# Sixteen attention heads' scores, minima and exps made inside the first layer's expert tiles

## The chip, the cores and the metric

One core of a Trainium2 chip runs the whole program in one launch. The metric is the device time of that core in microseconds, the median of several executions. TensorE does the matmuls and the transposes, VectorE (DVE in the profile) and ScalarE (ACT) the work on rows, GpSimd (POOL) the gathers by index, SyncE (SP) issues most DMAs. PSUM has eight banks of 128 partitions by 512 fp32 numbers, and TensorE writes nowhere else.

## What is computed

The network has two layers over 1024 tokens (4 sequences of 256) of width 256. Each layer multiplies an attention block by a gate from a mixture of experts; both read the same normalised rows.

```python
xn = _layernorm(x)
s = _L0_attn_ref(xn, Wq, Wk, Wv, Wo)          # softmax attention, 16 heads of 16, rope, causal
g = _silu(_L0_ffn_ref(xn, ...))               # 16 experts, the best 4 for each token
x = x + s * g
# second layer: linear attention and 32 experts, built in the same way

# inside _L0_ffn_ref, for each expert
gate = jnp.minimum(gate, LIMIT); up = jnp.clip(up, -LIMIT, LIMIT)
glu = gate * jax.nn.sigmoid(gate * ALPHA)
out = jnp.einsum('etd,edh->eth', (up + 1.0) * glu, down_proj) + down_proj_bias
out = (out * router_scores.T[:, :, None]).sum(axis=0)
# inside _L0_attn_ref
attn = jax.nn.softmax(where(causal, q @ k.T / 4, -inf)); out = attn @ v
```

With 4 sequences and 16 heads there are 64 heads to attend, each with a 256 by 256 causal matrix.

## The kernel before

Tokens are sorted by expert into rows of `NT0` = 47 tiles of 128. For each tile POOL gathers the rows, TensorE turns them (`turn`, bank 0 or 1), ACT copies them to SBUF (`turn`, L708), TensorE makes gate and up in 16 matmuls (`up`, L1169, bank 2 or 3), DVE adds biases and clips in four instructions and multiplies in a fifth (`gate`, L1642 to L1647), ACT makes the sigmoid (`gate`, L720), DVE multiplies by it (L1653), TensorE makes the down product in 4 matmuls (`down`, L1185, bank 6 or 7), and ACT weighs and stores it (`weigh`, L756). SP fetches each tile's expert weights four tiles ahead.

`run_tiles` writes out one order of work for each engine. For step u it goes through a list of (lag, every, work) and calls the work of tile u minus lag. TensorE's step u is: up of tile u-1, turn of tile u, down of tile u-3. ACT's step u is: turn of u, weigh of u-4, sigmoid of u-1, place heads, bias rows. DVE's is the gate of tile u-1. Engines work in their own order and meet only at semaphores, so whatever stands behind a waiting instruction waits too. POOL rotates queries and keys (rope) between the gathers of tiles 7 to 28; SP and ACT then place heads by DMA into `heads_qk`, the first half by tile 27.

When the tiles end, the attention starts, again in an order by steps, `run_pairs`: step u handles pairs of heads. `scores(n)` makes four heads' scores in 16 matmuls (L1264, banks 0 to 3), two for each head, packed by 32 rows of the array; for n of 1 or more it first waits until the minima of all four heads before are read out of the banks (`s_mx`, 8n). `smallest` on DVE masks and copies a head to SBUF and finds its minima (L1769, two instructions and their accumulator reads for each head), ACT makes the exps in place (`probs`, L835, two for each head), TensorE turns a head in three transposes (`turn_probs`, L1289, banks 4 and 5), DVE copies one head of the pair and ACT the other (L1778, L845), TensorE attends (`attend`, L1307, bank 6), and so on to the projection (L1334). Scores, minima and exps of pair p come in step p (the second exp in p+1), turning the pair in step p+2. Only `scores(0)` stands in the tile stretch, between the downs of its last two tiles. The ring of probabilities `pr` holds six heads.

Meanwhile POOL gathers the weighted rows back, 32 gathers (L595) that start when the last tile is stored; step 33 of DVE needs the last of them (`row_sums`). ACT holds the functions of one table at a time: `ahead` is a one-column activation that loads the next table early.

```python
def run_steps(total, body, stages):
    for u in range(min(lag for lag, _, _ in stages), total + max(lag for lag, _, _ in stages)):
        for lag, every, work in stages:
            v = u - lag
            if v % every == 0 and 0 <= v < total:
                work(v // every, v // every % (body // every))
```

## Time and profile before

| | us |
|---|---|
| median of 3 runs | 426.87 |
| lowest and highest | 425.85, 428.62 |
| span of the profiled execution | 462.5 |
| TensorE busy in it | 421.1 (91%) |
| VectorE busy in it | 329.8 (71%) |
| ScalarE busy in it | 234.4 (51%) |
| GpSimd busy in it | 216.2 (47%) |
| mean granted TensorE clock | 0.963 of 2.4 GHz |

The profiled execution is 35.6 us longer than the median of the plain runs. Times of instructions are read in it, and so a difference worked out from them is one in the profiled execution. An engine is busy while an instruction is in it; a matmul's end is modelled, and neighbours overlap, so start to start says more of TensorE than the duration. The granted clock is 1.00 at 2.4 GHz and 0.50 at 1.2 GHz.

### The profile page before, as it was taken

What the parts mean: (1) busy time and instruction counts of PE and PEld (TensorE: products, weight loads), DVE (VectorE), ACT (ScalarE), POOL (GpSimd) and SP (SyncE); (2) the same over time, 40 slices, a digit from 0 to 9 for tenths busy, and PEclk for the clock granted to TensorE, in tenths of its full rate; (3) what the DMA queues carried; (4) which work ended last, traced back from release to release, by engine and by line L of the source; (5) the groups of instructions that cost most, each with busy time, mean ns of one, the idle gap of its engine ahead of it and who ended that gap; (6) DMA issues with size and microseconds to landing.
All of it is one profiled execution on the core that took longest, in us unless ns stands there. A gap on an engine that the chain in (4) does not pass through costs nothing.

```text
span 462.5 us, 10086 instructions
## 1 busy us (share of the span) xinstructions
PE 421.1 (91%) x3213; PEld 327.6 (71%) x3213; DVE 329.8 (71%) x1135; ACT 234.4 (51%) x596; POOL 216.2 (47%) x208
## 2 busy tenths in 40 slices
PE   8899999899999998998989899958988999969696
PEld 4757899798999997656666684646766774645585
DVE  5886699978866667588999988525576664344685
ACT  3373233434433436878899636315566568124421
POOL 2023688767643320778880101655576602747400
PEclk9999999999999999589999999979999999979889
DMA  8937888888999982379776760233555523323202
GB/s 246 409 142 240 319 275 268 250 258 279 282 312 308 316 277 69 79 195 211 150 172 187 268 210 7 85 87 114 166 145 149 165 92 116 107 63 104 68 23 68
DMA packets 42274, 84.17 MB, mean 182 GB/s; under 512 B 7136, under 2 KB 27104, under 8 KB 41584
## 3 DMA queue, kind: packets, MB, share of 16 engines
q1 hardware_dynamic: 30656, 60.99, 39.6%
q0 software_dynamic: 9936, 20.85, 18.5%
q10 hardware_dynamic: 1632, 1.71, 1.1%
q8 instruction: 27, 0.44, 0.4%
q14 instruction: 23, 0.19, 0.1%
HBM read 65.81 MB, written 15.60 MB: 176 GB/s over the span
## 4 chain that ended last, share of the span: by engine, by line
PE 63%; DVE 14%; issue 8%; ACT 6%; another core or an unknown queue 4%; DMA 3%; SPq 1%; POOL 1%; ACTq 0%; DVEq 0%
PE ps L1169 14%; PE ps L1120 7%; PE ps L1185 7%; PE ps L1147 4%; PE ps L1289 4%; PE ps L964 3%; PE ps L1264 3%; PE ps L1106 3%; PE ps L1377 3%; ACT til L835 2%; PE ps L948 2%; PE ps L967 2%; DMA experts<-in_gu 2%; PE ps L1158 2%
## 5 line engine op out<-in xcount | busy, mean ns | idle before, releaser
L544 POOL DMA_INDIRECT til<-xn_rows,gidx x71 | 71.0, 999 | 98.1 <-PE ps L1158 43.4
L1169 PEld LDWEIGHTS ps<-til,experts 128*128 128x128 f32 x752 | 90.6, 192 | 8.1 <-issue 3.9
L1169 PE MATMUL ps<-til,experts 128*128 128x128 f32 x752 | 92.1, 276 | 3.2 <-DVE til L1645 1.5
L708 ACT ACTIVATE til<-ps 128x256 f32<-128x256 f32 x47 | 18.0, 382 | 66.2 <-PE ps L1158 66.2
L835 ACT ACTIVATE til<-til,mxs 128x128 f32<-128x128 f32 (+1 forms) x128 | 49.0, 453 | 0.0
L1185 PE MATMUL ps<-experts,til 128*128 x188 | 48.4, 381 | 0.0
L1120 PE MATMUL ps<-experts,til 128*64 x192 | 36.1, 345 | 9.4 <-issue 9.4
L756 ACT ACTIVATE til<-ps,wtile 128x256 f32<-128x256 f32 x95 | 42.0, 471 | 2.5 <-PE ps L1149 2.4
L1769 DVE CUSTOM_DVE_ANT_0 til<-ps,cst 128x128 f32<-128x128 f32 (+1 forms) x128 | 37.8, 352 | 5.7 <-PE ps L1264 3.3
L1120 PEld LDWEIGHTS ps<-experts,til 128*64 128x64 f32 x192 | 26.7, 144 | 15.5 <-issue 12.2
L1122 PE MATMUL ps<-xn,til 128*64 128x192 f32 x192 | 36.2, 345 | 0.0
L1289 PE MATMUL ps<-cst,til 128*128 128x128 f32 x192 | 31.3, 302 | 4.9 <-DVE til L1778 2.6
L1185 PEld LDWEIGHTS ps<-experts,til 128*128 128x128 f32 x188 | 32.1, 190 | 2.8 <-issue 0.3
L1289 PEld LDWEIGHTS ps<-cst,til 128*128 128x128 f32 x192 | 22.7, 152 | 15.5 <-issue 10.4
L544 POOL DMA_INDIRECT wqkv<-xn_rows,gidx x24 | 26.0, 1084 | 16.1 <-PE ps L1106 5.8
L1642 DVE TENSOR_SCALAR til<-ps,bcol 128x128 f32<-128x128 f32 x47 | 16.4, 348 | 23.9 <-PE ps L1169 23.0
L595 POOL DMA_INDIRECT rou<-sorted_rows,slotu x16 | 20.4, 1276 | 24.9 <-DMA sorted_rows<-til 19.4
L582 POOL DMA_INDIRECT rou<-sorted_rows,slotu x16 | 16.1, 1005 | 29.2 <-DMA sorted_rows<-til 20.3
L1660 DVE TENSOR_TENSOR til<-til,ps 128x192 f32<-128x192 f32 x24 | 8.5, 354 | 29.2 <-ACT til L727 22.5
L1366 PE MATMUL ps<-att,experts 128*128 128x512 f32 x64 | 29.0, 602 | 0.0
L1647 DVE SCALAR_TENSOR_TENSOR til<-til 128x256 f32<-128x256 f32 x47 | 27.9, 593 | 1.6
L1653 DVE TENSOR_TENSOR til<-til 128x256 f32<-128x256 f32 x47 | 27.1, 576 | 2.6 <-issue 0.5
(240 smaller groups left out, 959.4 us busy)
## 6 DMA issues: line engine op xcount, KB each, us to landing
experts<-in_gu SPq DMA_DIRECT2D x47, 512.0 KB
sorted_rows<-til SPq DMA_DIRECT2D x95, 128.0 KB
experts<-in_gu SPq DMA_DIRECT2D x8, 768.0 KB
experts<-in_dn SPq DMA_DIRECT2D x4, 1024.0 KB, 11.0
experts<-in_dn SPq DMA_DIRECT2D x8, 384.0 KB
experts<-att SPq DMA_DIRECT2D x44, 32.0 KB
til<-xn_rows,gidx POOLq DMA_INDIRECT x71
xr<-in_x SPq DMA_DIRECT2D x2, 512.0 KB, 4.2
```

Of the source, the lines that this page charges most:

```text
L544: po.indirect_dma_start(to, None, xn_dram[s.n], bass.IndirectOffsetOnAxis(ap=gidx[:, t:t + 1], axis=0))\
L756: ac.activation(ybuf[:, j, :], y, ACT.Copy, scale=wtile[:, t:t + 1])\
L835: ins = ac.activation(pr[h % len(pr)][:, cols], pr[h % len(pr)][:, cols], ACT.Exp, bias=mxs[:, h % len(pr), tt:tt + 1], scale=-1.0)
L1120: pe.matmul(ps[0:HALF_ROWS, 2 + p % 2, at], xgT1[:, p % 2, c, k, 0:HALF_ROWS], gu[:, bass.ds(e * (KD * w) + k * w, w)], start=(k == 0), st ...
L1122: mm = pe.matmul(ps[HALF_ROWS:P, 2 + p % 2, at], xgT1[:, p % 2, c, k, HALF_ROWS:P], gu_second[t % 4][:, k * w:(k + 1) * w], start=(k == 0) ...
L1169: mm = pe.matmul(ps[:, b0, m * P:(m + 1) * P], gw[:, j, k * w + m * P:k * w + (m + 1) * P], xgT[:, j % 2, k, :], start=(k == 0), stop=(k = ...
L1185: mm = pe.matmul(ps[:, 6 + j % 2, 0:D], hT[0:s.FP, j % 2, k, :], dn[0:s.FP, bass.ds(e * (s.KF * D) + k * D, D)], start=(k == 0), stop=(k = ...
L1289: mm = pe.transpose(ps[:, 4 + h % 2, n * P:(n + 1) * P], pr[h % len(pr)][:, n * P:(n + 1) * P], ident)
L1366: mm = pe.matmul(ps[:, n % 2 + 2 * w, :], wsgu_sb[:, k, w * SH + m * P:w * SH + (m + 1) * P], L[1].xnT[:, k, h * 512:(h + 1) * 512], start ...
L1647: ve.scalar_tensor_tensor(out=ubuf[:, j % 2, :], in0=ubuf[:, j % 2, :], scalar=1.0 - LIMIT, in1=gbuf[:, j % 2, :], op0=ALU.max, op1=ALU.mu ...
L1653: ve.tensor_tensor(hT[:, j % 2, :, :], ubuf[:, j % 2, :].rearrange("p (m t) -> p m t", m=2), sig[:, j % 2, :].rearrange("p (m t) -> p m t" ...
L1769: ve.tensor_tensor_reduce(out=pr[h % len(pr)][:, cols], in0=ps[:, h % 4, cols], in1=maskz[:, (1 - tt) * P:2 * P], scale=1.0, scalar=3.0e38 ...
```

## The change

Sixteen of the 64 heads (`AHEAD`, the first sequence) get their scores, minima and exps in the expert tiles' steps. TensorE's step gets `heads_ahead` at its end, `scores(0)` to `scores(3)` behind tiles 31, 35, 39 and 43; DVE's step gets `smallest_of_head` at its end, one head in each of tiles 32 to 45 and two in tile 46; ACT's gets `probs_ahead` at its end, one tile later. Banks for these scores are 1, 4, 5 and 7. For that, turns use bank 0 only and down products bank 6 only, so both wait for the copy of the tile just before, and ACT's `weigh` moves from second to first place in its step. The sigmoid becomes a Tanh of half the argument, its 1 is added in the last multiply (a SCALAR_TENSOR_TENSOR for the TENSOR_TENSOR), and the 0.5 goes into the tiles' weights; the two table loads around (Sigmoid, then Exp) go. Sixteen buffers for probabilities are laid in free memory, one of them new. In the attention the ring holds 14, and scores, minima and exps of the other 48 heads come four steps earlier against the turning than they did.

```diff
+        pr_ring = [til[:, 384 * n:384 * (n + 1)] for n in range(6)] + pr_ahead[8:16]
+        AHEAD = 16
+        AHEAD_TILE = 31
+        AHEAD_BANKS = (1, 4, 5, 7)
+        def heads_at(t):
+            h = t - AHEAD_TILE - 1
+            return () if h < 0 else (h, h + 1) if t == NT0 - 1 else (h,)
@@ ScalarE
-                ac.activation(ahead[:, :], ones_e[:, 0:1], (ACT.Sigmoid, ACT.Silu)[s.n])
+                if s.n == 1:
+                    ac.activation(ahead[:, :], ones_e[:, 0:1], ACT.Silu)
-                    ac.activation(sig[:, j % 2, 0:s.F], gbuf[:, j % 2, :], ACT.Sigmoid, scale=ALPHA)\
+                    ac.activation(sig[:, j % 2, 0:s.F], gbuf[:, j % 2, :], ACT.Tanh, scale=ALPHA / 2)\
-                    if s.n == 0 and t == NT0 - 3:
-                        ac.activation(ahead[:, :], ones_e[:, 0:1], ACT.Exp)
-                    run_tiles(s, [(0, 1, turn), (0, 1, last_wide), (4, 1, weigh), (1, 1, gate), (1, 1, place_heads), (2, 1, bias_rows)])
+                    run_tiles(s, [(4, 1, weigh), (0, 1, turn), (0, 1, last_wide), (1, 1, gate), (1, 1, place_heads), (2, 1, bias_rows), (2, 1, probs_ahead)])
+            def probs_of_head(h):
+                ac.wait_ge(s_mx, h * 2 + 2)
+                for tt, cols in ((0, slice(0, P)), (1, slice(P, 3 * P))):
+                    ins = ac.activation(probs_of(h)[:, cols], probs_of(h)[:, cols], ACT.Exp,
+                                        bias=mxs[:, h % 6, tt:tt + 1], scale=-1.0)
+                ins.then_inc(s_exp, 1)
-            run_pairs([(13, 8, ...), (1, 1, probs(1)), (2, 1, probs_turned_act),
-                       (8, 4, turned0), (0, 1, probs(0)), (4, 2, attended),
+            run_pairs([(13, 8, ...), (-3, 1, probs(1)), (2, 1, probs_turned_act),
+                       (8, 4, turned0), (-4, 1, probs(0)), (4, 2, attended),
@@ TensorE
-                    if t >= 2:
-                        pe.wait_ge(s.xgT_ready, t - 1)
+                    if t >= 1:
+                        pe.wait_ge(s.xgT_ready, t)
-                        mm = pe.transpose(ps[:, j % 2, k * P:(k + 1) * P], xg[:, j, k * P:(k + 1) * P], ident)
+                        mm = pe.transpose(ps[:, 0, k * P:(k + 1) * P], xg[:, j, k * P:(k + 1) * P], ident)
-                    if t >= 2:
-                        pe.wait_ge(s.y_ready, t - 1)
+                    if t >= 1:
+                        pe.wait_ge(s.y_ready, t)
-                        mm = pe.matmul(ps[:, 6 + j % 2, 0:D], hT[0:s.FP, j % 2, k, :],
+                        mm = pe.matmul(ps[:, 6, 0:D], hT[0:s.FP, j % 2, k, :],
-                    run_tiles(s, [(1, 1, up), ..., (3, 1, first_heads), (3, 1, down)])
+                    def heads_ahead(t, j):
+                        if t >= AHEAD_TILE and (t - AHEAD_TILE) % 4 == 0:
+                            scores((t - AHEAD_TILE) // 4, 0)
+                    run_tiles(s, [(1, 1, up), ..., (3, 1, down), (1, 1, heads_ahead)])
-                        mm = pe.matmul(ps[:, r, cols], ...)
+                        mm = pe.matmul(ps[:, AHEAD_BANKS[r] if n < AHEAD // 4 else r, cols], ...)
-            run_pairs([(0, 2, lambda n, j: scores(n, j) if n >= 1 else None), (2, 1, turn_probs), ...
+            run_pairs([(-4, 2, lambda n, j: scores(n, j) if n >= AHEAD // 4 else None), (2, 1, turn_probs), ...
@@ VectorE
-                    ve.tensor_tensor(hT[...], ubuf[...], sig[...], ALU.mult).then_inc(s.h_ready, 1)
+                    ve.scalar_tensor_tensor(out=hT[...], in0=sig[...], scalar=1.0,
+                                            in1=ubuf[...], op0=ALU.add, op1=ALU.mult).then_inc(s.h_ready, 1)
-                    run_tiles(s, [(1, 1, bias_columns), (1, 1, gate), (0, 1, weights(s)), (0, 1, bias_weights)])
+                    run_tiles(s, [(1, 1, bias_columns), (1, 1, gate), (0, 1, weights(s)), (0, 1, bias_weights), (1, 1, heads_ahead)])
-            run_pairs([(0, 1, smallest), (2, 1, probs_turned), ...
+            run_pairs([(-4, 1, smallest), (2, 1, probs_turned), ...
```

## Rows read from the trace of the kernel before

**Rows 1.** Windows by stage: start:end length, busy (instructions) PE PEld DVE ACT POOL, PEclk, DMA.
```profile
92.20:177.60 85.40, 84.80 (x646) 80.69 (x647) 63.15 (x174) 34.74 (x97) 38.51 (x42) 1.00 0.86 278
177.60:185.50 7.90, 6.49 (x62) 4.90 (x60) 5.39 (x25) 6.30 (x18) 0.00 (x0) 1.00 0.26 86
185.50:201.50 16.00, 15.42 (x125) 10.24 (x121) 10.63 (x56) 12.25 (x35) 12.04 (x9) 0.57 0.61 137
201.50:247.80 46.30, 41.34 (x491) 28.27 (x487) 42.05 (x202) 41.13 (x118) 34.05 (x25) 1.00 0.79 181
247.80:259.40 11.60, 10.22 (x115) 7.27 (x111) 11.30 (x51) 10.26 (x29) 1.05 (x1) 1.00 0.67 227
```

**Rows 2.** Timeline of one expert tile: start, length, engine, line, operation, idle before it.
```profile
166.14 1.95 PE L1169 MATMUL ps<-til,experts 128*128 128x128 f32 x16
...
168.12 0.35 DVE L1642 TENSOR_SCALAR til<-ps,bcol 128x128 f32<-128x128 f32 x1 [0.82 <-PE ps L1169]
168.14 1.03 PE L1185 MATMUL ps<-experts,til 128*128 x4
168.34 0.38 ACT L708 ACTIVATE til<-ps 128x256 f32<-128x256 f32 x1 [1.81 <-PE ps L1158]
...
168.62 0.47 ACT L756 ACTIVATE til<-ps,wtile 128x256 f32<-128x256 f32 x1
...
169.01 1.95 PE L1169 MATMUL ps<-til,experts 128*128 128x128 f32 x16
...
169.74 0.42 DVE L1653 TENSOR_TENSOR til<-til 128x256 f32<-128x256 f32 x1
```

**Rows 3.** Timeline from the last tile's gate and up to the first turned heads.
```profile
177.61 1.95 PE L1169 MATMUL ps<-til,experts 128*128 128x128 f32 x16
...
181.34 1.28 ACT L761 ACT_TABLE_LOAD   x1
...
183.84 0.28 DVE L1769 CUSTOM_DVE_ANT_0 til<-ps,cst 128x128 f32<-128x128 f32 x1
...
184.07 2.86 ACT L835 ACTIVATE til<-til,mxs 128x128 f32<-128x128 f32 x8
184.40 0.08 DVE L1769 DVE_READ_ACCUMULATOR2_ANT mxs<- 128x1 f32 x1
...
184.63 0.94 PE L1264 MATMUL ps<-experts 16*128 16x128 f32 x16 [1.41 <-DVE mxs L1769]
...
185.50 1.29 PE L1289 MATMUL ps<-cst,til 128*128 128x128 f32 x6
```

**Rows 4.** Page, costliest groups: the two multiplies of the expert gate, all 47 tiles.
```profile
L1647 DVE SCALAR_TENSOR_TENSOR til<-til 128x256 f32<-128x256 f32 x47 | 27.9, 593 | 1.6
L1653 DVE TENSOR_TENSOR til<-til 128x256 f32<-128x256 f32 x47 | 27.1, 576 | 2.6 <-issue 0.5
```

**Rows 5.** Timeline, TensorE: turned heads at steps 8, 28 and 33 of the attention.
```profile
201.47 0.87 PE L1289 MATMUL ps<-cst,til 128*128 128x128 f32 x6
...
247.80 0.87 PE L1289 MATMUL ps<-cst,til 128*128 128x128 f32 x6
...
259.38 0.88 PE L1289 MATMUL ps<-cst,til 128*128 128x128 f32 x6
```

**Rows 6.** Timeline, GpSimd (last gather back) and ScalarE (a Tanh among the exps).
```profile
241.27 1.53 POOL L595 DMA_INDIRECT experts<-sorted_rows,slotu  x1 [0.30 <-issue]
...
213.32 0.63 ACT L859 ACTIVATE rou<-rou 128x512 f32<-128x512 f32 x1
```

**Rows 7.** Windows of 2 us around a fall and a rise of the clock, later in the kernel.
```profile
304.00:306.00 2.00, 0.60 (x4) 0.33 (x3) 0.00 (x0) 0.00 (x0) 0.47 (x1) 0.82 0.40 117
...
312.00:314.00 2.00, 2.00 (x20) 1.21 (x16) 1.20 (x5) 1.03 (x3) 0.00 (x0) 0.98 0.20 55
```

**Rows 8.** TensorE: a gap in the second layer's tiles, and 2 us around it.
```profile
323.26 0.37 PE L1120 MATMUL ps<-experts,til 128*64 x1 [1.37 <-issue]
...
322.00:324.00 2.00, 0.74 (x10) 0.69 (x12) 2.00 (x7) 2.00 (x6) 1.65 (x2) 1.00 0.52 145
```

More of the change, by code:

```diff
@@ L170, in build_program @@
         dn_second = [wo0_sb[0:F1, n, :] for n in range(2)] + [xn_free[0:F1, 1536 + n * D:1536 + (n + 1) * D] for n in range(2)]
-        pr = [til[:, 384 * n:384 * (n + 1)] for n in range(6)]
+        pr_more = sb("pr_more", [P, 384])
         prT = [til[:, 384 * n:384 * (n + 1)] for n in range(6, 9)] + [big[:, 14336 + 384 * n:14336 + 384 * (n + 1)] for n in range(5)]
@@ L241, in build_program @@
         shift1 = (rou[:, 2048:3072].rearrange("p (t n) -> p t n", t=4), stk.rearrange("p a w t -> p (a w) t"))
+        xnT0_free = att[:, 6144:8192]
+        pr_ahead = ([rou[:, 2048 + 384 * n:2048 + 384 * (n + 1)] for n in range(4)]
+                    + [stk[:, 1, :, :].rearrange("p w t -> p (w t)")[:, 0:384], pr_more[:, :]]
+                    + [xn_free[:, 384 * n:384 * (n + 1)] for n in range(5)] + [xnT0_free[:, 384 * n:384 * (n + 1)] for n in range(5)])
+        pr_ring = [til[:, 384 * n:384 * (n + 1)] for n in range(6)] + pr_ahead[8:16]
         mxs = sb("mxs", [P, 6, 2])
@@ L398, in build_program, with probs_of @@
         EARLY_ROWS = ((0, 4), (4, 6), (6, 8))
+        AHEAD = 16
+        AHEAD_TILE = 31
+        AHEAD_BANKS = (1, 4, 5, 7)
+        def probs_of(h):
+            return pr_ahead[h] if h < AHEAD else pr_ring[(h - AHEAD) % len(pr_ring)]
+        def heads_at(t):
+            h = t - AHEAD_TILE - 1
+            return () if h < 0 else (h, h + 1) if t == NT0 - 1 else (h,)
+        assert [h for t in range(NT0) for h in heads_at(t)] == list(range(AHEAD))
         ONCE = BATCH * HEADS // 2
@@ L832, in work @@
                     h = 2 * p + half
-                    ac.wait_ge(s_mx, h * 2 + 2)
-                    for tt, cols in ((0, slice(0, P)), (1, slice(P, 3 * P))):
-                        ins = ac.activation(pr[h % len(pr)][:, cols], pr[h % len(pr)][:, cols], ACT.Exp,
-                                            bias=mxs[:, h % len(pr), tt:tt + 1], scale=-1.0)
-                    ins.then_inc(s_exp, 1)
+                    if h >= AHEAD:
+                        probs_of_head(h)
                 return work
@@ L1221, in tiles @@
                 if s.n == 0:
-                    def first_heads(t, j):
-                        if t == NT0 - 1:
-                            scores(0, 0)
-                    run_tiles(s, [(1, 1, up), (0, 1, turn), (0, 4, experts), (0, 1, begin), (1, 1, weights), (1, 1, bias_rows), (3, 1, first_heads), (3, 1, down)])
+                    def heads_ahead(t, j):
+                        if t >= AHEAD_TILE and (t - AHEAD_TILE) % 4 == 0:
+                            scores((t - AHEAD_TILE) // 4, 0)
+                    run_tiles(s, [(1, 1, up), (0, 1, turn), (0, 4, experts), (0, 1, begin), (1, 1, weights), (1, 1, bias_rows), (3, 1, down), (1, 1, heads_ahead)])
                 else:
@@ L1283, in turn_probs @@
             def turn_probs(p, j):
+                if p == 0:
+                    pe.wait_ge(s_mx, 2 * AHEAD)
                 for h in (2 * p, 2 * p + 1):
@@ L1710, in tiles, with heads_ahead @@
                 if s.n == 0:
-                    run_tiles(s, [(1, 1, bias_columns), (1, 1, gate), (0, 1, weights(s)), (0, 1, bias_weights)])
+                    def heads_ahead(t, j):
+                        if t == AHEAD_TILE + 3:
+                            ve.wait_ge(s_rope, NTT)
+                        for h in heads_at(t):
+                            smallest_of_head(h)
+                    run_tiles(s, [(1, 1, bias_columns), (1, 1, gate), (0, 1, weights(s)), (0, 1, bias_weights), (1, 1, heads_ahead)])
                 else:
@@ L1748, in tiles, with smallest_of_head @@
                     run_double_tiles([(0, first_copies), (1, turned_four), (0, gate_four), (0, copy_four), (1, biases), (3, products)])
+            def smallest_of_head(h):
+                ve.wait_ge(s_sc, h + 1)
+                if h >= 6:
+                    ve.wait_ge(s_exp, h - 5)
+                if h >= AHEAD + 6:
+                    ve.wait_ge(s_pT, h - len(pr_ring) + 1)
+                bank = AHEAD_BANKS[h % 4] if h < AHEAD else h % 4
+                for tt, cols in ((0, slice(0, P)), (1, slice(P, 3 * P))):
+                    ve.tensor_tensor_reduce(out=probs_of(h)[:, cols], in0=ps[:, bank, cols], in1=maskz[:, (1 - tt) * P:2 * P],
+                                            scale=1.0, scalar=3.0e38, op0=ALU.add, op1=ALU.min,
+                                            accum_out=mxs[:, h % 6, tt:tt + 1]).then_inc(s_mx, 1)
             link(ve.memset(ones_e[:, :], 1.0))
@@ L1764, in smallest @@
                 for h in (2 * p, 2 * p + 1):
[L1765 to L1771 removed]
+                    if h >= AHEAD:
+                        smallest_of_head(h)
             def probs_turned(p, j):
```

32 lines of the change are left out of this document (15 added, 17 removed).

## The prediction

> **What bounds the kernel now.** I read the windows by stage first, because a mean over the span mixes stretches with different limits. From 92 us to the last expert tile TensorE is busy 84.80 of 85.40 us and DVE 63.15 [rows 1]: this stretch goes at TensorE's pace, and everything added to TensorE's order there is paid in full. The attention is another thing. From 201.5 to 247.8 us DVE is busy 42.05 of 46.3, TensorE 41.34 and ACT 41.13 [rows 1]: three engines at about 90%, none of them free. The 16 us before that ran at a granted clock of 0.57. If the clock has only the levels 1.00 and 0.50, that is 13.8 us at 1.2 GHz (0.86 of 16.0), with TensorE busy 15.42 us [rows 1]. So the change takes work from a stretch where all three are loaded and gives it to one where DVE and ACT have room and TensorE has none.
>
> The timeline of one tile comes second. Call T the start of an up. The next up starts at T+2.87, DVE starts the gate at T+1.98, and its last multiply ends at T+4.02 (169.74 + 0.42 against 166.14) [rows 2]. DVE thus needs 2.04 us of 2.87. The timeline of the hand-over comes third: from the last up (177.61) to the first turned head (185.50) go 7.9 us, with a TensorE gap of 1.41 us that DVE's minima end [rows 3].
>
> **The edits that cost nothing.** One bank for turns: the up of tile t already waits for the same copy (L708), and TensorE's next turn stands behind that up, so the new wait is always fulfilled. One bank for downs: down of tile t now waits for weigh of t-1. ACT turns at T+2.20, makes the tanh, then in the last tiles two exps (0.72 a head: 2.86 for eight [rows 3]), then weighs (0.47 [rows 2]). All four are 0.38 + 0.42 + 0.72 + 0.47, about 2.0 us, taking a tanh like DVE's multiply of as many columns; they end near T+4.2, or T+1.3 of the next tile, and down comes there at T+2.0, right behind the up and the turn (168.14 [rows 2]). It has 0.7 us to spare, and if that went, it would add to each tile. The other multiply: a SCALAR_TENSOR_TENSOR of the same columns costs 27.9 us for 47 against 27.1 [rows 4], at most 0.8 in all; I take 0. Tanh for Sigmoid: a Tanh stands among exps with no table load before it [rows 6], so Tanh and Exp can alternate. The removed load at 181.34 is 1.28 us of ACT [rows 3]; its gain is in the hand-over below. The other removed load lies before the tiles, where TensorE sets the pace: 0 (bounds 0 and -1.3).
>
> **The scores in the tiles.** Four `scores`, 0.87 us each (184.63 to 185.50 [rows 3]), are 3.5 us on the engine that bounds. DVE's added head takes 0.64 us (183.84 to 184.48 [rows 3]), 2.68 with the gate, under 2.87: DVE keeps up.
>
> Then the wait. `scores(n)` needs the minima of head 4n-1. That head's minima stand in DVE's step for tile 31+4n, behind the gate of this tile, and this gate needs the up of the same tile. `scores(n)` stands in TensorE's step of the same tile. So TensorE, done with turn and down at T+2.87, stands until DVE has ended the gate (T+4.02), the head (0.64) and the signal has passed (184.48 to 184.63, 0.15 [rows 3]): T+4.81. That is 1.94 us of waiting, for n = 1, 2 and 3, and the next up is behind it in TensorE's order, then everything that waits for it. `scores(0)` has no such wait. Sum of the stretch: 4 x 0.87 + 3 x 1.94 = 9.3 us. Bounds: without waits 3.5, with 2.3 us each 10.4; I take 9.3, since its parts are read next to each other.
>
> **The hand-over.** From the last up: gate ends at 4.02, DVE's two heads (14 and 15) at 5.3, ACT's exps of head 15 at 6.0, then weigh of tile 45 (0.47), down of tile 46 (0.87), which needs it in the one bank: 7.4, first turned head at 7.5 against 7.9 before. -0.4. TensorE has one up and three downs in this time, so it stands idle for more than 2.5 us. I expect the clock to fall here as it did before.
>
> **The attention**, from first turn to the turn of step 33. Before: 185.50 to 259.38, 73.9 us [rows 3, 5]. Steps 2 to 8 took 16.0. Steps 2 and 3 now hold no scores, minima or exps; I take 1.5 off for the two (a scores at each level of the clock would be 0.87 and 1.7) and leave the rest at the low clock: 14.5 (bounds 12.4 with a high clock, at 2.3 a step, and 16.0). Steps 8 to 28 took 46.3. They hold the same work as before, because what moved is the head start: 24 pairs still need their minima and exps by step 27. The exps are no longer fresh when the turn comes, so a little waiting goes: 45.5 (bounds: DVE's own 42.1, and 46.3). Steps 28 to 33 took 11.6 [rows 5] and lose a scores and the last exps. TensorE's own work there is 10.22 busy less 0.87, 9.3 [rows 1]; I take 9.6 (bounds 9.3, 11.6). Sum 69.6, which is -4.3. TensorE's work over all of it is 8.8 (15.42 at 0.57) + 41.3 + 10.2 - 1.7 = 58.6 us at full clock and 65.5 with 13.8 us of it at half: 69.6 is 94% of that, so there is not much more to get while the clock is low. The gathers don't bind: the last is issued at 242.8, 57.3 us after the first turn [rows 6, 3], and step 33 comes at 69.6.
>
> **Sum.** +9.3 - 0.4 - 4.3 = +4.6 us on the profiled span of 462.5. The plain runs are 35.6 us shorter and I can't see where; I carry the difference over unchanged: 426.9 + 4.6 = 431.5 us, 1.1% slower.
>
> **Rivals.**
>
> The clock falls in the tiles. A gap of 1.37 us left the clock at 1.00 in the second layer [rows 8]; a gap of 1.41 us followed by scores was followed by the fall at the hand-over [rows 1, 3]. The waits here are 1.94 us and followed by scores too, which speaks for it; for the rest of the four tiles TensorE is dense, which speaks against it. A low spell in the second layer ran from 305.3 to 312.1 by the means 0.82 and 0.98, 6.8 us [rows 7], and costs 3.4 us where TensorE bounds. Three falls: +10.2, 441.7 us; one: 434.9.
> The Trainium skill, "TensorE: Matmul & The Clock Gate", section "A second HAM failure mode: psum-queue depth-cycling", says that a kernel that cycles through PSUM banks and lets TensorE idle briefly between groups of matmuls can swing between both clock levels. That is the pattern which this change makes in the tiles; by that rule the sum is the rival's 441.7, and the row of the 1.37 us gap does not agree with it.
>
> The attention comes free of its bound, and the kernel is faster. The mechanism: with 16 heads' probabilities ready, the first turns come in an unbroken row, TensorE keeps or soon regains 2.4 GHz, and DVE sets the pace. DVE's busy time in the attention is 10.63 + 42.05 + 11.30 = 64.0 us [rows 1], less 12 heads by 0.64, 56.3. (Four heads lay before the first turn already.) At the 91% of the long window this is 61.9 us, at the 97% of the last one 58.0; TensorE's 58.6 stands beside it. Net 9.3 - 0.4 - 12.0 = -3.1, 423.8 us, and at best 7.0 less, 419.9. The point from which it decides: an attention below 65.0 us makes up for the tiles. Against it: two downs spaced by waits stand right before the turns, and TensorE was busy 15.42 of 16 us before and still had the low clock.
>
> The waits are not there. If something hides them, 3.5 - 0.4 - 4.3 = -1.2, 425.7 us, no change. Only a gate that DVE could finish before TensorE's down would do that, and 4.02 against 2.87 speaks plainly against it.
>
> **How the numbers follow.** Forecast 52%, with its own range of 427.5 to 436 (waits of 1.5 to 2.3 us, attention of 66 to 73); clock falling in the tiles 15%; attention unbound 23%; waits absent 10%. A measurement of this kernel can tell about 1% from no change, 4.3 us. Slower by over 1%: 28 of the forecast's 52 (its middle lies just over the line), the 15 and 3 of the rest, 46%. Within 1%: 24, 10 of the unbound attention, 5, 39%. Faster: 13 and 2, 15%. The range reaches from 421.5, where nearly all of the unbound attention is in, to 440, with two falls of the clock in.
>
> **What would show it.** In the timeline of the changed kernel: TensorE idle for about 1.9 us before three of the four early `scores`, ended by DVE's accumulator read; tile starts 5.7 us apart there and 2.87 elsewhere. The window from 92 us to the last tile's up 9.3 us longer, at clock 1.00. From the last up to the first turned head about 7.5 us; a clock near 0.5 behind it. From the first turn to step 33's about 70 us. It is wrong in the tiles if the waits are short or the clock is below 1.00 there, in the attention if it takes under 66 us, and in the carrying over if the profiled spans differ by 4 to 5 us and the medians do not.

## The result, and the profile after

| | before | after |
|---|---|---|
| median, us | 427.55 | 447.67 |
| lowest and highest | 425.85, 428.62 | 446.14, 449.91 |
| ratio after / before, 95% interval | | 1.0446 (1.0405 to 1.0486) |
| span of the profiled execution | 462.5, and 425.9 in a second one | 446.9 |

The changed kernel is slower by 20.1 us, where 4.6 had been forecast. On another chip the same two kernels gave 449.13 against 427.9 (below).

The kernel before was profiled again (`before_again`): 427.73 us, span 425.9. Its first profile, on which the prediction rests, was an unusually slow execution, so the comparison is made with the second. The windows by stage of it, the counterpart of [rows 1] and the stages behind (start:end, length, busy time of TensorE, its weight loads, VectorE, ScalarE and GpSimd with instructions, granted clock, share of the DMA engines, GB/s):

```profile
92.20:133.10 40.90, 40.90 (x316) 39.38 (x316) 33.70 (x84) 17.56 (x48) 26.42 (x29) 1.00 0.90 288
133.10:176.20 43.10, 43.10 (x332) 41.51 (x332) 29.72 (x92) 17.09 (x51) 12.04 (x14) 1.00 0.84 277
176.20:184.00 7.80, 6.39 (x61) 4.85 (x59) 5.33 (x25) 6.20 (x18) 0.00 (x0) 1.00 0.27 87
184.00:200.00 16.00, 14.84 (x153) 10.15 (x150) 12.92 (x72) 14.40 (x42) 11.95 (x9) 0.79 0.63 139
200.00:251.90 51.90, 47.91 (x570) 33.73 (x568) 50.28 (x240) 49.03 (x139) 34.88 (x26) 1.00 0.86 211
251.90:270.50 18.60, 17.84 (x130) 15.26 (x127) 16.29 (x70) 7.23 (x20) 1.88 (x2) 1.00 0.62 202
```

The same view of the changed kernel, cut at the same events of the work:

```profile
92.20:138.40 46.20, 43.32 (x326) 40.73 (x325) 35.67 (x90) 21.27 (x50) 28.09 (x30) 1.00 0.86 273
138.40:192.40 54.00, 49.18 (x396) 44.83 (x395) 36.87 (x144) 27.60 (x74) 11.94 (x14) 0.97 0.69 213
192.40:200.90 8.50, 5.81 (x30) 4.44 (x29) 4.71 (x21) 5.44 (x16) 0.00 (x0) 0.84 0.14 46
200.90:216.90 16.00, 15.63 (x151) 10.55 (x149) 10.97 (x56) 11.29 (x32) 9.89 (x8) 0.77 0.58 135
216.90:267.00 50.10, 45.77 (x535) 32.70 (x534) 45.66 (x206) 43.74 (x122) 36.92 (x27) 1.00 0.87 209
267.00:291.20 24.20, 20.86 (x131) 17.66 (x127) 16.23 (x70) 7.34 (x20) 1.40 (x2) 0.86 0.56 185
```

The cuts are the up of tile 31, the last up, the first turned head, the turn of step 33, and layer two's first wide product. Between them stand the 21.0 us by which the two profiled spans differ:

| stage | before, us | after, us | difference | predicted |
|---|---|---|---|---|
| start to up of tile 31 | 133.1 | 138.4 | +5.3 | 0 |
| up of tile 31 to last up | 43.0 | 54.0 | +10.9 | +9.3 |
| last up to first turned head | 7.9 | 8.5 | +0.6 | -0.4 |
| attention, to the turn of step 33 | 67.9 | 66.2 | -1.7 | -4.3 |
| to layer two's first wide product | 18.6 | 24.2 | +5.6 | 0 |
| the rest of layer two | 155.4 | 155.7 | +0.3 | 0 |

TensorE fills both of the first windows of before (40.90 of 40.90, 43.10 of 43.10). After, it stands idle for 2.9 and 4.8 us there. In the second it has the scores to make besides; the first holds slightly more of the tiles' work, since both views begin at 92.20 and the changed kernel is 3.2 us late by then (tile 17's up at 95.18 against 92.02). TensorE's waits from 38 to 200 us, changed kernel (waiting line, releaser, us in total, times, longest):

```profile
PE ps L1211 <- ACT til L776: 6.8, 6, 1.5
PE ps L1292 <- DVE mxs L1796: 4.8, 3, 1.6
PE ps L1195 <- DMA experts<-in_gu: 1.3, 1, 1.3
```

L1292 is the scores in the tiles and L1211 the down product, which was L1185 in [rows 2]. In the second profile of before, TensorE waits 1.5 us for VectorE and 0.3 us for expert weights in these tiles, and for nothing else.

**The second tile of scores.** TensorE's timeline there, the counterpart of [rows 2] (start, length, engine, line, operation, idle before it):

```profile
152.96 1.03 PE L1211 MATMUL ps<-experts,til 128*128 x4
155.60 0.94 PE L1292 MATMUL ps<-experts 16*128 16x128 f32 x16 [1.60 <-DVE mxs L1796]
156.46 3.13 PE L1195 MATMUL ps<-til,experts 128*128 128x128 f32 x16
159.38 0.63 PE L1184 MATMUL ps<-cst,til 128*128 128x128 f32 x2
159.81 1.44 PE L1211 MATMUL ps<-experts,til 128*128 x4
161.08 1.95 PE L1195 MATMUL ps<-til,experts 128*128 128x128 f32 x16
...
155.46 0.08 DVE L1796 DVE_READ_ACCUMULATOR2_ANT mxs<- 128x1 f32 x1
```

and a window of 2 us in the next tile:

```profile
158.00:160.00 2.00, 2.00 (x11) 2.00 (x11) 0.37 (x2) 0.00 (x0) 0.00 (x0) 0.50 0.05 18
```

The wait is where the prediction put it, and VectorE's accumulator read ends it. Behind it one up takes 3.13 us instead of 1.95: TensorE's clock fell to its lower level (0.50 in the window), and this tile lasts 4.62 us, where the tiles behind the other scores take 2.97: 1.65 us lost. The waits of 1.61 us before the scores at 171.46 and at 185.68 were followed by ups of the usual length.

**The end of the attention.** The chain of waits (start, us, what):

```profile
260.01 1.53 POOL experts L614
261.54 0.30 issue
261.85 10.62 DMA experts<-sorted_rows,slotu
272.59 0.69 DVE rou L1838
273.48 0.43 DVE stk L1830
273.96 0.69 PE ps L1356 x2
```

and the two lines of the timeline that belong to it:

```profile
272.59 0.69 DVE L1838 TENSOR_TENSOR rou<-rou,experts 128x512 f32<-128x512 f32 x1 [3.26 <-DMA experts<-sorted_rows,slotu]
...
273.96 0.69 PE L1356 MATMUL ps<-cst,stk 128*128 128x128 f32 x2 [2.59 <-DVE stk L1830]
```

The last gather was issued at 261.85, 61.0 us after the first turned head, and its rows were used 10.6 us later. VectorE waited 3.26 us for them in `row_sums` of the last sequence, the normalisation of the same sums stands behind it, and TensorE waited 2.59. In this last window TensorE's clock is 0.86 with 20.86 us busy, against 1.00 and 17.84 before: 3.0 us of the stage's 5.6 are the clock that fell behind the wait, 2.6 the wait. In `before_again` the last gather is issued at 242.60 and the same sum starts at 254.20, 11.6 us later, with no wait.

### The profile page after: what moved, and what is told of

The parts are those of the page before. It is cut to its first block, busy times and chain, and to the rows that moved or that the text cites. A ratio compares the mean times of both kernels' runs of the same rounds, so it can differ in the third digit from the quotient of the medians.

```text
span 446.9 us, 10085 instructions
## 1 busy us (share of the span) xinstructions
PE 416.4 (93%) x3213; PEld 325.8 (73%) x3213; DVE 332.1 (74%) x1135; ACT 239.6 (54%) x592; POOL 213.6 (48%) x208
## 3 DMA queue, kind: packets, MB, share of 16 engines
q0 software_dynamic: 9936, 20.85, 18.1%
## 4 chain that ended last, share of the span: by engine, by line
PE 61%; DVE 12%; DMA 12%; POOL 6%; issue 4%; ACT 2%; SPq 1%; ACTq 1%; POOLq 0%; DVEq 0%
PE ps L1195 14%; DMA experts<-sorted_rows,slotu 8%; PE ps L1146 6%; PE ps L1211 6%; PE ps L1396 6%; PE ps L1173 4%; PE ps L990 3%; PE ps L1407 3%; PE ps L1132 3%; POOL experts L614 3%; PE ps L974 2%; POOL rou L614 2%; DVE til L1677 2%; DMA experts<-in_gu 2%; PE ps L993 2%
## 5 line engine op out<-in xcount | busy, mean ns | idle before, releaser
L1211 PE MATMUL ps<-experts,til 128*128 x188 | 50.8, 394 | 7.0 <-ACT til L776 6.8
L1211 PEld LDWEIGHTS ps<-experts,til 128*128 128x128 f32 x188 | 32.9, 195 | 12.3 <-issue 9.5
L1148 PE MATMUL ps<-xn,til 128*64 128x192 f32 x192 | 33.8, 329 | 0.0
L1146 PE MATMUL ps<-experts,til 128*64 x192 | 33.7, 329 | 0.0
L740 ACT ACTIVATE til<-til 128x256 f32<-128x256 f32 x47 | 19.6, 417 | 20.7 <-DVE til L1673 19.3
L1677 DVE SCALAR_TENSOR_TENSOR til<-til 128x256 f32<-128x256 f32 x47 | 29.2, 622 | 1.6
L1683 DVE SCALAR_TENSOR_TENSOR til<-til 128x256 f32<-128x256 f32 x47 | 27.0, 575 | 3.6 <-PE ps L1211 2.2
L614 POOL DMA_INDIRECT experts<-sorted_rows,slotu x16 | 25.2, 1576 | 9.0 <-DMA experts<-sorted_rows,slotu 5.0
L563 POOL DMA_INDIRECT wqkv<-xn_rows,gidx x24 | 24.4, 1018 | 10.2 <-issue 5.8
L601 POOL DMA_INDIRECT rou<-sorted_rows,slotu x16 | 15.4, 965 | 24.0 <-DMA sorted_rows<-til 19.4
L1148 PEld LDWEIGHTS ps<-xn,til 128*64 128x64 f32 x192 | 25.3, 137 | 0.0
L1173 PE MATMUL ps<-experts,til 96*64 x96 | 22.7, 379 | 0.5 <-ACT til L776 0.5
L1292 PE MATMUL ps<-experts 16*128 16x128 f32 (+1 forms) x256 | 15.7, 362 | 5.8 <-DVE mxs L1796 5.8
## 6 DMA issues: line engine op xcount, KB each, us to landing
experts<-in_dn SPq DMA_DIRECT2D x4, 1024.0 KB, 11.7
```

Of the source, the lines that this page charges most:

```text
L563: po.indirect_dma_start(to, None, xn_dram[s.n], bass.IndirectOffsetOnAxis(ap=gidx[:, t:t + 1], axis=0))\
L614: po.indirect_dma_start(rows[:, i, :], None, ys_dram[s.n], bass.IndirectOffsetOnAxis(ap=slotu[s.n][:, i * TOPK + k:i * TOPK + k + 1], axis=0),
L740: ac.activation(sig[:, j % 2, 0:s.F], gbuf[:, j % 2, :], ACT.Tanh, scale=ALPHA / 2)\
L1146: pe.matmul(ps[0:HALF_ROWS, 2 + p % 2, at], xgT1[:, p % 2, c, k, 0:HALF_ROWS], gu[:, bass.ds(e * (KD * w) + k * w, w)], start=(k == 0), st ...
L1148: mm = pe.matmul(ps[HALF_ROWS:P, 2 + p % 2, at], xgT1[:, p % 2, c, k, HALF_ROWS:P], gu_second[t % 4][:, k * w:(k + 1) * w], start=(k == 0) ...
L1173: pe.matmul(ps[0:HALF_ROWS, 6 + p % 2, at], hT1[:, p % 2, c, 0:HALF_ROWS], dn[0:F1, bass.ds(e * D, D)], start=True, stop=True)
```

## The experiments

Twelve runs follow, two of them repeats. Differences in us are between medians; the kernel before had 427.6 to 429.3 on the chips they ran on, so the ratio to it is given too. The diffs are abridged: the reading side of a moved bank, changed semaphore counts and lines without weight for the argument are left out.

**The kernel before again.**

> The kernel before, unchanged, for a second profile of it. The first profiled execution had a span of 462.5 us where plain runs took 427. If that execution was an odd one, this profile has a span near 426 us and differs from the first mostly behind 300 us, in the second layer's tiles; then all comparisons behind 300 us go against this one. If profiling itself stretches this kernel, the span is again near 460 us.

Measured: 427.73 us, span 425.9. Its windows stand in the section above.

**The changed kernel again.**

> The changed kernel once more, unchanged, beside the kernel before on the same chip, as the reference for the runs with one edit undone. If its 447.7 us against 427.6 hold on another chip, the ratio is 1.0446 within 0.4%, about 448 us beside 429, and the three single edits (9.5, 4.7 and 5.4 us) sum to 19.6 where the three together gave 18.1. If the first time was high by the chip it ran on, the ratio is near 1.040 and the sum of the single edits falls to that of the three together.

Measured: 449.13 us, ratio 1.0489 (1.0454 to 1.0524), before 427.9. The loss is not one chip's, and if anything it is larger. In this profile tile 36 takes its usual 2.97 us behind the wait before `scores(1)`, and the low clock comes behind the wait before `scores(2)` instead (tile 40 lasts 4.62 us there, 2.97 in the first profile). The three variants below that keep the waits show one fall (`after_late_weights`, tile 36), one (`after_two_down_banks`, tile 44) and two (`after_fewer_gathers`, tiles 36 and 44): 6 falls behind 15 waits of 1.6 us in five profiles. Two more things differ from the first profile. TensorE waits 2.2 us for expert weights at tile 4 and tile 4 then lasts 4.59 us, and the attention takes 64.8 us with a clock of 0.95 in its first 16 us, where the first profile had 66.2 and 0.77.

**The waits taken away.** Scores one tile later (the lag goes from 1 to 2; expectations further down call it two), when the minima are already there:

```diff
-  run_tiles(s, [(1, 1, up), ..., (3, 1, down), (1, 1, heads_ahead)])
+  run_tiles(s, [(1, 1, up), ..., (3, 1, down), (2, 1, heads_ahead)])
```

> The changed kernel with its four early score groups one step later in TensorE's order, so that the minima they need are already made. Theory 1 (three causes add up: waits before the scores, one bank for the downs, the gathers back at the end of the attention): the three waits of 1.6 to 1.7 us and the clock's fall behind the first of them (1.8 us) go, 6.7 us of the tile stretch, and because the gathers set the end of the attention and start with the last tile, nearly all of it arrives: 441 us. Theory 2 (what was lost lies behind the tiles alone, in the attention and its clock): under 2 us less than the changed kernel's 447.7. Theory 3 (TensorE's added work counts, not its waits): same as the changed kernel.

Measured: 438.22 us, ratio 1.0194 (1.0147 to 1.0240), 9.5 us less than the changed kernel. The window of the last tiles of layer one, and that of the first 16 us of the attention:

```profile
138.00:188.00 50.00, 50.00 (x417) 45.91 (x416) 38.64 (x149) 28.82 (x77) 12.76 (x15) 1.00 0.78 248
...
195.60:211.60 16.00, 14.75 (x189) 10.14 (x187) 12.91 (x67) 13.77 (x40) 10.01 (x8) 1.00 0.64 170
```

TensorE has no gap in the tiles. The 4.8 us of waits and the 1.65 us of the slow tile go, and from the up of tile 31 to the last up it is 47.3 us instead of 54.0. Two things more are shorter in this profile: the hand-over is 7.6 us instead of 8.5, and the clock is 1.00 instead of 0.77 in the first turns, so that the attention takes 63.4 us instead of 66.2. How much of this is the edit's is less sure: the changed kernel's own clock in these 16 us differs between executions (0.77 and 0.95). The profiled execution is also the slowest of the four, 441.5 us; it waited 2.4 us for expert weights at tile 4.

**Two banks for the down products** of the first 28 tiles (bank 7 is given to the scores only from tile 31 on):

```diff
+  ONE_BANK = 28
+  def down_bank(t): return 6 + t % 2 if t < ONE_BANK else 6
-  if t >= 1: pe.wait_ge(s.y_ready, t)
+  if t >= 2: pe.wait_ge(s.y_ready, t - 1 if t < ONE_BANK else t)
-  mm = pe.matmul(ps[:, 6, 0:D], ...)
+  mm = pe.matmul(ps[:, down_bank(t), 0:D], ...)
```

> The changed kernel with two banks for the down products of tiles 0 to 27, one from tile 28 on. Theory 1: in the stretch where GpSimd rotates and VectorE is late (tiles 4 to 26), down waits for the weighing of the tile just before, which stands behind the late gate in ScalarE's order; two banks give back up to 3.2 us of the 3.8 lost by tile 31: 444.5 us. Rival: the loss in this stretch comes from the new multiply (a SCALAR_TENSOR_TENSOR beside GpSimd's rotations) or from ScalarE weighing first; then the tiles 0 to 31 are as late as in the changed kernel and the time stays within 1 us of 447.7.

Measured: 443.0 us, ratio 1.0333 (1.0270 to 1.0395), 4.7 us less. The up of tile 31 starts at 134.61 instead of 138.42; from there to the last up it is 53.96 us in both, as it should be, for both have one bank there. What one bank costs in the last tiles this run can't tell; in the changed kernel's list of waits no down waits between 138 and 192 us, and the next run, without the heads, has 43.0 us there as before. The attention is 1.7 us shorter in this profile (64.5 us, clock 0.94 in its first 16 us), but so it is in a variant that is the same as the changed kernel up to there (64.4 us, 0.94, in `after_fewer_gathers`). Of the 3.8 us at tile 31, 0.7 stood already at the first up (38.76 against 39.46). From the up of tile 5 to that of tile 31 the changed kernel takes 82.3 us, this one 78.8 and `before_again` 77.9: 3.5 us belong to the bank, and 0.9 us stay with two banks, their cause not tested.

**One bank on the kernel before**, for turns and for downs, with ScalarE's weighing first; heads and gate as before:

```diff
-  mm = pe.transpose(ps[:, j % 2, ...], ...)        # waits for xgT_ready, t - 1
+  mm = pe.transpose(ps[:, 0, ...], ...)            # waits for xgT_ready, t
-  mm = pe.matmul(ps[:, 6 + j % 2, 0:D], ...)       # waits for y_ready, t - 1
+  mm = pe.matmul(ps[:, 6, 0:D], ...)               # waits for y_ready, t
-  run_tiles(s, [(0, 1, turn), (0, 1, last_wide), (4, 1, weigh), ...])
+  run_tiles(s, [(4, 1, weigh), (0, 1, turn), (0, 1, last_wide), ...])
```

> The kernel before with one part of the change alone: in layer one one bank for the turns and one for the down products, and ScalarE's weighing of the products first among its steps. Heads and gate stay as before, the work is whole. Theory one (the single bank costs most of the 4.7 us that came back with two banks, in tiles 13 to 31 where VectorE's part of the gate runs late beside GpSimd's rotations): the last up product comes 3 to 5 us later and the time is 427.6 + 3 to 5 = 430.5 to 432.5. Theory two (the bank costs only together with the work that the heads add in the last tiles, or the hand-over): at most 1.5 us longer, 427.6 to 429.

Measured: 432.37 us, ratio 1.0085 (1.0040 to 1.0130), 3.1 us more than before on that chip. In the profile the tiles are 4.5 us longer by tile 31 than in `before_again` and not at all after it. From the up of tile 5 to that of tile 31 it takes 82.3 us, exactly what the changed kernel takes, so heads and gate have no part in this stretch. Five steps of 0.5 to 1.0 us, before the ups of tiles 14 to 26, make 3.9 of the 4.5. The hand-over is 1.0 us longer too (8.9 us) and the attention 1.9 shorter (66.0 us, at a clock of 1.00 against 0.79 in its first 16 us), which is why the median moves by less than the tiles. The timeline of the first, between the ups of tiles 13 (77.98) and 14 (82.60), on GpSimd, VectorE, TensorE and ScalarE:

```profile
76.86 1.34 POOL L571 TENSOR_TENSOR att<-att,experts 128x512 f32<-128x512 f32 x1
77.11 1.37 DVE L1653 TENSOR_TENSOR til<-til 128x256 f32<-128x256 f32 x1
...
77.98 1.95 PE L1169 MATMUL ps<-til,experts 128*128 128x128 f32 x16
...
78.41 0.88 DVE L1598 CAST experts<-rou 128x384 bf16<-128x384 f32 x1
...
79.32 0.70 DVE L1599 TENSOR_TENSOR rou<-rou,experts 128x128 f32<-128x128 f32 x1
...
80.32 0.34 DVE L1643 TENSOR_SCALAR til<-ps,bcol 128x128 f32<-128x128 f32 x1
...
80.70 0.42 ACT L720 ACTIVATE til<-til 128x256 f32<-128x256 f32 x1 [3.13 <-DVE til L1643]
...
81.02 0.46 ACT L756 ACTIVATE til<-ps,wtile 128x256 f32<-128x256 f32 x1
...
81.64 1.13 PE L1185 MATMUL ps<-experts,til 128*128 x4 [1.49 <-ACT til L756]
```

Read it upwards. TensorE's down waits for the weighing (L756). The weighing stands behind the sigmoid (L720) in ScalarE's order, the sigmoid waits 3.13 us for VectorE's bias and clip (L1643), and VectorE comes to tile 12's gate 5.1 us after the start of its up (80.05 against 74.97), where in a quiet tile it is 2.0 [rows 2]. It is late with a multiply that takes 1.37 us beside GpSimd's rotations, where it takes 0.42 in a quiet tile, and with a cast and a subtraction that split the routing weights. Before the change VectorE was late at this place too, but TensorE had one more bank to go on with, and waited less, for VectorE before its next up (`before_again`):

```profile
82.03 2.02 PE L1169 MATMUL ps<-til,experts 128*128 128x128 f32 x16 [0.83 <-DVE til L1645]
```

This run holds three edits at once, the two banks and ScalarE's order. That the down products' bank has most of the cost is told by the run before it; the other two were not tried alone. The Trainium skill, "GPSIMD Engine Reference", section "Specifications", says that VectorE and GpSimd share their interfaces to SBUF and that VectorE's instructions with two SBUF inputs contend; the 1.37 against 0.42 us agree.

**The last gathers taken away.** The last four of the 32 gathers are left out, so the last sequence's gate lacks part of its rows; on both kernels:

```diff
-  for r in range(2):
+  for r in range(2 if b < BATCH - 1 else 1):
```

> The changed kernel without the last four of the 32 gathers back (the second half of the experts' sum for the last sequence is left out, so its gate is wrong). Theory 1: at the end of the attention VectorE stands 3.3 us for the last gather's landing, TensorE and ScalarE behind it, and the clock falls for about 8 us; without four gathers of 1.8 us the sum is ready before it is asked for, 3.3 us of waiting and about 4 us of low clock go: 440 us. Rival (the end of the attention is bound by the engines, and the wait only takes the place of another): under 2 us less.

Measured: 441.66 us, ratio 1.0270 (1.0218 to 1.0321), 6.0 us less. No wait before the sum, and 18.6 us from step 33 to layer two instead of 24.2.

> The kernel before without the last four of the 32 gathers that bring the experts' rows back (the sums of the last sequence's second half then lack that part of the data; nothing else is left out). Theory one (before, the engines' work in the attention ends within about 1 us of the gathers, so the gathers bind only once the attention is shorter): the time is 0 to 1.5 us lower, 426 to 427.6, against 6.0 us that the same edit gave on the changed kernel. Theory two (the gathers bound the kernel before as much): 4 us lower or more, 423.5.

Measured: 428.02 us, ratio 0.9962 (0.9932 to 0.9993), 1.2 us less than before on that chip. The gathers bind the kernel before by 0.3 to 2.9 us, less than half of what they take from the changed one.

**The weights out of the gathers' way.** SP's order, on both kernels:

```diff
   sp.wait_ge(s_sc, BATCH * HEADS)
+  sp.wait_ge(s_sum, BATCH)
   for c in (5, 6, 7): gate_up_columns(c)
-  sp.wait_ge(s_sum, BATCH)
```

> The changed kernel with SP's wait for the last attention sums moved ahead of the loads of gate_up columns 5, 6 and 7, which are issued at 259.6 us in the changed kernel, while the last gathers are under way. The work is whole. Theory one (these loads share the DMA engines with the last gathers, which land 10.6 us after issue): the last gather lands sooner, the wait before row_sums(3) of 3.26 us goes to under 1 us, and the time falls by 2 to 4 us, if layer two's tiles do not then wait for columns 5 to 7. Theory two (the gathers are bound by their own transfers and by when they start): the wait stays within 0.7 us of 3.26, and the time is the same or longer by what the late columns cost.

Measured: 442.25 us, ratio 1.0290 (1.0229 to 1.0351), 5.4 us less; more than expected, because the clock stays up too. SP's issues (four of 768 KB: column 4, which no edit moves, and the three loads) and the 12 us up to step 33 in the changed kernel:

```profile
259.61 2.00 SPq L507 DMA_DIRECT2D experts<-in_gu  x4
...
255.00:267.00 12.00, 11.16 (x121) 8.27 (x120) 10.00 (x35) 8.12 (x22) 7.34 (x7) 1.00 1.00 279
```

The same with the loads held back, with the sum and the stage behind step 33:

```profile
258.39 12.04 SPq L507 DMA_DIRECT2D experts<-in_gu  x4
...
254.00:266.00 12.00, 11.16 (x122) 8.30 (x115) 10.00 (x34) 7.96 (x22) 7.30 (x6) 1.00 0.82 184
...
268.12 0.69 DVE L1838 TENSOR_TENSOR rou<-rou,experts 128x512 f32<-128x512 f32 x1
...
265.80:284.40 18.60, 17.84 (x130) 15.26 (x127) 16.30 (x70) 7.23 (x20) 1.88 (x2) 1.00 0.79 285
```

Column 4 goes out at 258.39 here too, the three loads from 268.91 on. The sum starts 7.3 us after the last gather's issue (260.79) instead of 10.6, with no wait at all, and the stage is 18.6 us, as before the change. Of the 12 us up to step 33 the DMA engines are busy for all in the changed kernel (share 1.00), and for 0.82 here. So the wait in the changed kernel was a collision: both the gathers' last rows and three loads of 768 KB want the DMA engines at one moment. Before the change they missed each other: in `before_again` the three loads are issued from 245.80 on, 3.2 us behind the last gather (242.60), in the changed kernel from 260.00 on, 1.9 us ahead of it (261.85). The Trainium skill, "DMA: Bandwidth & Descriptors", section "SWDGE vs HWDGE vs iDMA", says that each DMA engine goes round between the queues that GpSimd's and the other engines' transfers feed; a gather then slows when SP's queue is filled as well, and this pair of runs agrees.

> The kernel before with SP's wait for the last attention sums moved ahead of the loads of gate_up columns 5 to 7. The work is whole. Theory one (before, nothing waits for the last gather, and the late columns cost nothing): the same time, within 1 us of 428, and the stage from the last turned group to layer two's first wide product stays at 18.6 us. Theory two (the loads slow the gathers before too, and the attention follows them): 1.5 to 5 us faster.

Measured: 428.0 us, ratio 0.9992 (0.9969 to 1.0015): no difference. Before, nothing waits for these rows, and later columns cost nothing.

**Two and three edits together.**

> The changed kernel with both of TensorE's orders undone at once: the heads' scores are tried two tiles later, so that nothing is waited for, and down products of layer one's first 28 tiles use banks 6 and 7 in turn. The work is whole. Theory one (two stalls of different places: the three waits of 1.6 us with the clock that fell behind them, and the single down bank): the gains of the two runs add, 9.5 + 4.7 = 14.2 us, and the time is 447.7 - 14.2 = 433.5, between 432 and 435. Theory two (both free the same slack, what one gives is in part what the other gives): the gain is that of the larger alone with at most 1 us beside it, 437 to 438.

Measured: 433.32 us, ratio 1.0106 (1.0061 to 1.0151), 14.4 us less than the changed kernel.

> The changed kernel with all three edits together: scores tried two tiles later, two down banks in the first 28 tiles, and SP's wait for the last attention sums ahead of the loads of gate_up columns 5 to 7. The work is whole. The two first gave 433.3 us, the third alone 5.4 us. Theory one (the wait for the last gather's rows, 23.3 us from the last turned group to layer two's first wide product against 18.6, comes from these loads): that stage is 18.6 us again and the time is 433.3 - 4.7 = 428.6, within 1 us of the kernel before, 427 to 430, because 4.5 us of shorter attention and 3.5 us of added scores nearly cancel. Theory two (with the attention 63.4 us long instead of 66.2 the gathers' own issues bind as well): at least 1.5 us of wait stays, 430 to 432.

Measured: 429.58 us, ratio 1.0046 (1.0013 to 1.0080), 18.1 us less. Three parts account for nearly all of the loss, and what is left is 1.1 us (0.6 to 3.4 by the interval). Windows from 2 us ahead of the first turn (188.94) on, the rest to near step 33, and the end:

```profile
187.00:203.00 16.00, 14.80 (x158) 10.53 (x158) 11.12 (x58) 11.76 (x34) 8.74 (x7) 0.91 0.52 134
203.00:250.00 47.00, 43.52 (x510) 31.35 (x510) 43.05 (x198) 42.31 (x119) 36.19 (x27) 1.00 0.85 198
250.00:268.60 18.60, 17.55 (x139) 14.48 (x138) 16.97 (x68) 7.59 (x21) 3.39 (x5) 1.00 0.73 250
```

Its stages against `before_again`: 4.3 us more from tile 31 to the last up (four scores by 0.87, and 0.8), 0.6 in the hand-over, 4.4 less in the attention (63.5), nothing at its end. The trade as such is nearly even in these runs; part of the 4.4 is the clock of the first turns, which was 0.79 in `before_again`. The single edits' gains of 9.5, 4.7 and 5.4 us come to 1.5 us more than the three together, and by the ratios to more: 5.2% of the kernel before against 4.0%, some 5 us. Two reasons can be named, and no run weighs them: the clock in the first turns can be gained only once (the attention takes 63.4 us without the waits and 63.4 without the waits and with two banks), and the clock also differs between executions.

**The gate alone**, on the kernel before: Tanh of half the argument, the fused add and multiply, weights halved, no table loads (the last two are left out of the diff).

```diff
-  ac.activation(sig[...], gbuf[...], ACT.Sigmoid, scale=ALPHA)
+  ac.activation(sig[...], gbuf[...], ACT.Tanh, scale=ALPHA / 2)
-  ve.tensor_tensor(hT[...], ubuf[...], sig[...], ALU.mult)
+  ve.scalar_tensor_tensor(out=hT[...], in0=sig[...], scalar=1.0, in1=ubuf[...], op0=ALU.add, op1=ALU.mult)
```

> The kernel before with the gate of layer one by tanh alone (the fused add and multiply on VectorE, the weights halved, no loads of the two function tables). The work is whole. Theory one (ScalarE and VectorE are not what layer one's tiles wait for, and the last table load lies beside TensorE's last products): the same time within 1 us of 428, hand-over 0 to 1.3 us shorter. Theory two (the table load before the first exps is on the path of the hand-over, and the gate's longer instruction on that of the tiles): a change by more than 1.5 us either way.

Measured: 428.05 us, ratio 0.9992 (0.9962 to 1.0022): no difference. Its hand-over is 7.9 us as before; the table load was beside other work.

## Why the prediction was right in its direction and wrong in its size

**The waits in the tiles: right in kind, the total partly by luck.** Four scores, three waits and none before the first, each ended by VectorE's accumulator read. The waits were 1.60 and 1.61 us instead of 1.94: the down ends at T+3.03 and the minima at T+4.58, where the sum had 2.87 and 4.66. A scores, on the other hand, costs 1.07 us in the tiles and not 0.87 (47.3 us without waits against 43.0). Without the 1.65 us of the clock the stretch gained 9.3 us, as forecast; waits priced 1.0 us too high and scores 0.8 us too low cancel.

**The clock in the tiles: a rival, and it came in part.** The prediction gave 15% to it and 3.4 us to a fall. In the changed kernel it was one fall in each of two profiles, at different waits, 1.65 us each. The rule that stood with this rival (the Trainium skill, "TensorE: Matmul & The Clock Gate", section "A second HAM failure mode: psum-queue depth-cycling") holds in kind; neither it nor the row of the 1.37 us gap [rows 8] says which wait is followed by a fall.

**"It has 0.7 us to spare": the step that failed first**, +4.5 us. Both edits that halved a ring of banks were priced at nothing. For the turns nothing speaks against it: L1184 appears in no list of waits. For the downs the slack was worked out in one quiet tile at 166 us [rows 2] and then taken for all 47. In the tiles in which GpSimd rotates and VectorE works on lists, VectorE's bias and clip come up to 3 us later, ScalarE's sigmoid waits for them, and the weighing stands behind the sigmoid. The row that would have told it was on the prediction's own page: both multiplies of the gate have a mean of 593 and 576 ns [rows 4], where one in the quiet tile takes 420; so some take far longer. The run with banks and order alone on the kernel before confirms it: +4.5 us in its profile's tiles, +3.1 us between the medians.

**"The gathers don't bind": the second**, +5.6 us. The prediction compared the issue of the last gather (57.3 us after the first turn) with step 33 (69.6). The rows are there only when they have landed, and that took 10.6 us: 61.0 + 10.6 = 71.6 us after the first turn, when VectorE wanted them at 68.5. It also left out that the change pulls SP's next loads forward: they wait for the last scores, which now come four steps earlier against the turning. Counted from the first turn the three loads are issued 59.1 us on instead of 61.8, and the last gather 61.0 us on instead of 58.6, so that they change places. With the loads held back the stall is gone though the gathers start no sooner. The start was no help either: the first gather goes out when the last tile is stored, 11.7 us after the last up (204.12) and not 8.8 as in `before_again`, since the last downs wait and run at the low clock.

**The hand-over**: 8.5 us instead of 7.5. The timeline shows the two last downs waiting 1.44 and 1.25 us for the weighing, which stands behind exps of 0.78 to 1.49 us in ScalarE's order, and the last down at the low clock (2.07 us for four matmuls). The sum had held the parts, but not the second wait; the fall of the clock it had expected, and priced the last down at full speed.

**The attention**: 66.2 us, at the lower end of the forecast's 66 to 73 and quicker than its 69.6, and yet a gain of only 1.7 us. The reference was wrong. [Rows 1 and 5] come from an execution in which the attention took 73.9 us with a clock of 0.57 in its first 16 us; in other profiles of the kernel before, or of near copies, it takes 66.0 to 68.6 us with clocks of 1.00 to 0.70. Taken at the same clock of 1.00, heads made ahead save 66.0 - 63.4 = 2.6 us (`before_one_bank` against `after_no_waits`), less than the 4.3 us that four scores cost in the tiles. One reading in this part is turned round: TensorE's 65.5 us are 94% of 69.6, not the other way.

**The carried-over difference**: 35.6 us stood between the profile and the plain runs, and the prediction said that it could not see where. Against the second profile the first one is 1.5 us longer by the last up, 6 us in the attention, 15.4 in layer two's tiles (90.0 us from 294.76 to 384.76, against 74.6) and 13.6 behind them (77.7 against 64.1). The sum was carried over unchanged, as if the slow stretches had no part in what was being priced. The attention was one of them.

**The rivals**: the attention unbound would have needed under 65.0 us. It came to 66.2 in the changed kernel, to 64.8 in its second profile, and to 63.4 once the waits were gone, so the mechanism is there (`after_no_waits`, clock 1.00 from the first turn), but its worth was counted from 73.9 and not from 67.9: the second profile is under 65.0, and the kernel was 21 us slower all the same. But the clock of these turns is not fixed by the schedule: four profiles with the same work up to there (the changed kernel twice, `after_late_weights`, `after_fewer_gathers`) show 0.77, 0.95, 0.76 and 0.94 with 66.2, 64.8, 66.0 and 64.4 us. "Waits absent" did not happen.

**Left open.** TensorE waits 0.9 to 2.4 us for the expert weights near tile 4 in six profiles of the changed kernel and its variants (0.7 us with three edits, none with two), 1.1 us in the first profile of the kernel before, and 0.4 us or less in the five others of it and its variants. It is part of the 5.3 us at tile 31 (about 0.9), and no run was made on it. Behind the waits of 2.2 and 2.4 us the tile lasts 4.59 and 4.35 us, behind those of 1.3 and 1.7 us 2.94 and 2.95. Why the clock falls behind 6 of 15 equal waits, and behind other ones each time, no run here settles. The same holds for the clock of the first turns.

## What to carry to other kernels

A ring of buffers has slack in the worst step, not in the mean one: before halving it, look for the steps in which the engine that frees it is late, and follow what stands behind what in that engine's order. Price a transfer to its landing, with all that will be in the DMA queues at that moment after the change, for a shorter stage moves the next stage's loads too. And where the profiled execution is 8% longer than the plain runs, ask for the stretch that is long before taking a gain out of it.

## What the hardware showed that was not expected

The rows of the last indirect gather were there 7.3 us after its issue, or sooner, with one load of 768 KB issued 2.4 us ahead of it, and 10.6 us after it with three more such loads. A multiply of 128x256 on VectorE took 0.42 us in a quiet tile and 1.37 us beside GpSimd's rotations. A wait of 1.6 us followed by scores was followed by 1.2 GHz in 6 of 15 cases, and a fall cost 1.65 us in the tile. At the end of the attention a fall cost about as much as the wait ahead of it, 3.0 us behind 2.6. The same kernel's attention took 67.9 us in one execution and 73.9 in another, with a granted clock in its first 16 us of 0.79 and 0.57.
